# Transposing the MLP's pre-activation instead of computing it a second time, in the first phase of a two-layer decoder kernel

## The reference

```
z    = x @ w1.T + b1                # 512 hidden features
pred = silu(z) @ w2.T + b2
e    = pred - v
grad_w2, grad_b2  from e and silu(z)
dz   = (e @ w2) * silu'(z),  grad_w1, grad_b1  from dz and x
w   <- (1 - alpha) * w - theta * grad
```

## Time and profile before

| what | value |
|---|---|
| median of three runs | 1011.18 us (1008.25 to 1017.53) |
| the profiled execution's own time | 1009.8 us |
| its span | 1008.1 us |
| mean granted TensorE clock, share of full speed | 0.863 |
| busy: PE / DVE / ACT / POOL | 745.5 / 527.1 / 383.9 / 163.0 us |
| TensorE's weight loads (PEld), beside PE | 481.1 us |
| first phase | 0 to 270 us |
| gradient loop of step 0 / 1 / 2 / 3, from its first product | 59.68 / 125.96 / 186.21 / 248.73 us |

### The profile page before, as it was taken

The page is one execution under the profiler, slowest core; times in us unless marked ns, Lnnn a source line. Parts: engine busy times, 40 slices in busy tenths (PEclk is TensorE's granted clock), DMA queues, the critical chain, the costliest instruction groups (busy, mean ns, idle before and its releaser), DMA issues.

```text
span 1008.1 us, 13899 instructions
## 1 busy us (share of the span) xinstructions
PE 745.5 (74%) x4570; PEld 481.1 (48%) x4570; DVE 527.1 (52%) x1934; ACT 383.9 (38%) x888; POOL 163.0 (16%) x207
## 2 busy tenths in 40 slices
PE   5788796887865986985984972999357568667665
PEld 4445354453422662662662751778336336344342
DVE  4435245252625945945946821111245784876865
ACT  3514436144222542542540541333024354344543
POOL 9300000000111005005004004000331411311020
PEclk8889899898966997997995985999787889788887
DMA  7500000010024026026024001141110100200000
GB/s 213 181 1 21 2 21 0 10 42 0 11 48 105 1 49 100 11 47 98 12 44 55 2 1 61 27 108 44 48 40 2 46 7 13 52 11 12 0 12 10
DMA packets 49246, 39.49 MB, mean 39 GB/s; under 512 B 11235, under 2 KB 42659, under 8 KB 49189
## 3 DMA queue, kind: packets, MB, share of 16 engines
q1 hardware_dynamic: 47140, 34.62, 15.7%
q0 software_dynamic: 2048, 4.20, 1.5%
HBM read 27.20 MB, written 11.60 MB: 38 GB/s over the span
## 4 chain that ended last, share of the span: by engine, by line
PE 54%; DVE 23%; issue 8%; ACT 7%; DMA 5%; SPq 2%; POOL 1%; DVEq 0%; ACTq 0%; POOLq 0%
PE bank L1247 4%; PE bank L1236 4%; PE bank L1349 3%; DVE R L2182 3%; DMA q_stack<-parts_dram 3%; PE bank L1130 2%; PE bank L990 2%; PE bank L1133 2%; PE bank L1143 2%; PE bank L1132 2%; PE bank L922 2%; DVE bank L1900 2%; PE bank L1102 2%; PE bank L1013 2%; PE bank L1050 2%
## 5 line engine op out<-in xcount | busy, mean ns | idle before, releaser
L1900 DVE CUSTOM_DVE_ANT_0 bank<-bank,add_q 128x256 f32<-128x256 f32 x256 | 100.1, 456 | 34.7 <-PE bank L1102 21.6
L1558 ACT ACTIVATE pT<-bank 128x512 f32<-128x512 f32 x128 | 76.1, 597 | 75.7 <-PE bank L1133 73.4
L1102 PE MATMUL bank<-k_stack,q_stack 96*128 96x256 bf16 x256 | 51.7, 300 | 31.0 <-DMA q_stack<-parts_dram 24.2
L1349 PE MATMUL bank<-XT,kpad 128*128 128x256 f32 (+1 forms) x256 | 60.8, 368 | 15.9 <-DVE cT L2124 15.9
L1130 PE MATMUL bank<-q_stack,k_stack 96*128 96x256 bf16 x256 | 70.3, 275 | 1.8 <-DVE mx L1900 1.8
L1132 PE MATMUL bank<-add_k,ident_b 128*128 128x256 bf16 x256 | 70.6, 276 | 0.0
L1133 PE MATMUL bank<-neg_max,head_sel 96*128 96x256 bf16 x256 | 70.5, 275 | 0.0
L1349 PEld LDWEIGHTS bank<-XT,kpad 128*128 128x128 f32 x256 | 49.9, 217 | 26.1 <-DVE cT L2124 17.7
L2124 DVE TENSOR_TENSOR cT<-bank,decay 128x384 f32<-128x384 f32 x64 | 35.1, 554 | 48.5 <-POOL decay L872 28.3
L1583 ACT ACTIVATE he<-bank 128x324 f32<-128x324 f32 x64 | 28.2, 441 | 69.4 <-PE bank L1236 63.9
L872 POOL TENSOR_SCALAR_AFFINE_SELECT decay<-decay 128x256 f32<-128x256 f32 x64 | 27.2, 426 | 159.5 <-ACT decay L1652 159.5
(11 more groups left out here) (412 smaller groups left out, 1680.8 us busy)
## 6 DMA issues: line engine op xcount, KB each, us to landing
k_stack<-parts_dram SPq DMA_DIRECT2D x48, 64.0 KB
q_stack<-parts_dram SPq DMA_DIRECT2D x24, 128.0 KB, 8.1
expert_in<-no_rows SPq DMA_DIRECT2D x8, 324.0 KB, 4.0
rows<-expert_in SPq DMA_DIRECT2D x8, 324.0 KB
expert_out<-rows_y SPq DMA_DIRECT2D x8, 324.0 KB
moe_w<-in_L_ffn_w_dram SPq DMA_DIRECT2D x1, 2048.0 KB
parts_dram<-k_parts SPq DMA_DIRECT2D x4, 384.0 KB, 2.8
parts_dram<-q_parts SPq DMA_DIRECT2D x12, 128.0 KB, 1.7
```

What stands on the lines that cost most here:

```text
L1102: last = pe.matmul(q_bank(n)[:, c * S:(c + 1) * S], q_stack[:, h // 2, b * S + c * P:b * S + (c + 1) * P], k_stack[:, h // 2, h % 2, b * S ...
L1349: last = pe.matmul(c_bank(n)[:, lo:lo + width], kpad2[:, h, b * S + c * P:b * S + (c + 1) * P], XT[:, par, q0:q0 + width], start=True, sto ...
L1558: act.activation(pT[:, g % 2, j], k_bank(n)[:].rearrange("p (c q) -> p c q", c=QC), ACT.Exp).then_inc(exp_ready.sem, 1)
L1900: last = dve.tensor_tensor_reduce(sc, sc, add_q[:, b * QC + c, :], 1.0, 2.0 * NEG, ALU.add, ALU.max, mx[:, c, h:h + 1])
```

## The change

z in feature layout, bias included, now stays in a tile of its own, zs, 512 + 64 tokens wide; hT gets silu of it. `z_and_dh` fills its PSUM bank by four transposes of 128 x 128 blocks of zs instead of the f32 product and the bias product. The bias parts go: their tiles, their DMA, their zeroing, VectorE's five instructions and TensorE's wait for them. VectorE's wait for masks_made stands after the first phase now. In step 0 ScalarE writes the memory tokens' z by four Identity activations, waits for its own last one, and then takes four Silu; z_copied counts one more there, and TensorE waits for it in step 0 ahead of the loop.

```diff
--- before.py
+++ after.py
@@ -208,19 +208,18 @@
         swa_ready = signal("swa_ready", 1, extra=1)
         vT_copied = signal("vT_copied", 1, extra=1)
         zT_a = signal("zT_a", FC, extra=1)
-        z_copied = signal("z_copied", FC)
+        z_copied = signal("z_copied", FC, extra=1)
         hT_a = signal("hT_a", FC, extra=FC)
         pred_a = signal("pred_a", 1)
         e_ready = signal("e_ready", 1)
         eT_tr = signal("eT_tr", 1)
         etok_copied = signal("etok_copied", 1, extra=1)
         zd_ready = signal("zd_ready", NC, extra=1)
-        b1_split = signal("b1_split")
         sg_ready = signal("sg_ready", NC, extra=1)
         dz_ready = signal("dz_ready", NC, extra=1)
         grads_ready = signal("grads_ready", NC, extra=1)
         grads_added = signal("grads_added", 1)
-        dve_a = signal("dve_a", 2 * NU + 2 * NC, extra=2 + 1 + 2 + 3)
+        dve_a = signal("dve_a", 2 * NU + 2 * NC, extra=2 + 1 + 2)
         upd_pe = signal("upd_pe")
         upd_dve = signal("upd_dve")
         updated = signal("updated")
@@ -407,10 +406,7 @@
         grad1 = sb("grad1", [P, HID], scope=scope_a)
         grad2 = sb("grad2", [P, HID], scope=scope_a)
         grad_b = sb("grad_b", [P, FC + 1], scope=scope_a)
-        b1_row = sb("b1_row", [1, HID], scope=scope_a)
-        b1_rest = sb("b1_rest", [1, HID], scope=scope_a)
-        b1_mid = sb("b1_mid", [1, HID], BF16, scope=scope_a)
-        b1_parts = sb("b1_parts", [96, HID], BF16, scope=scope_a)
+        zs = sb("zs", [P, FC, T + M], scope=scope_a)
 
         stage = ExitStack()
         qT = sb("qT", [P, T], scope=stage)
@@ -587,7 +583,6 @@
             (w2T[:], a["L0_attn_w2T"].rearrange("(k p) d -> p k d", p=P)),
             (b1[:], a["L0_attn_b1_cols"]),
             (b2[:], a["L0_attn_b2"].unsqueeze(1)),
-            (b1_row[:], a["L0_attn_b1"].unsqueeze(0)),
             (rate[:, 0:1], a["L0_attn_alpha"].partition_broadcast(P)),
             (rate[:, 1:2], a["L0_attn_theta"].partition_broadcast(P)),
             (xtok[0:M, NC, :], a["L0_attn_mem"]),
@@ -787,7 +782,7 @@
             pool.iota(iota_e[:], pattern=[[1, E]], base=0, channel_multiplier=0, allow_small_or_imprecise_dtypes=True)
             pool.iota(first_slot[:], pattern=[[SLOTS, E]], base=0, channel_multiplier=0, allow_small_or_imprecise_dtypes=True)
             pool.iota(trash[:], pattern=[[P, PAIRS]], base=E * SLOTS, channel_multiplier=1, allow_small_or_imprecise_dtypes=True)
-            for t in (b1_parts, q_stack, k_stack, neg_max, neg_pm, v_aug, seen, fb_parts):
+            for t in (q_stack, k_stack, neg_max, neg_pm, v_aug, seen, fb_parts):
                 pool.memset(t[:], 0.0)
             pool.memset(ones16[:], 1.0)
             made = Chain(pool, masks_made, 0)
@@ -946,7 +941,7 @@
                     pe.wait_ge(*pTb_copied.at(i, u + 1))
                     wait_apart(pe, passed, *pTa_copied.at(i, u + 1))
                     if c is None:
-                        pe.wait_ge(*z_copied.at(i))
+                        pe.wait_ge(*z_copied.at(i, FC))
                     heads = [(h, slice(DH0 * h, DH0 * h + DH0)) for h in range(H0)]
                     if c is None:
                         for h, r in heads:
@@ -1009,12 +1004,13 @@
                         pe.wait_ge(*dz_ready.at(i, c - 2))
                     if c >= 2:
                         pe.wait_ge(*sg_ready.at(i, c - 1))
-                    x_c = xin[:, c // QC, M + (c % QC) * P:M + (c % QC + 1) * P] if c < NC else xin[:, 0, 0:M]
-                    pe.matmul(zb[0:n], x_c, w1T[:], start=True, stop=False)
-                    pe.matmul(zb[0:n], row_sel[:, 0:n], b1_parts[:], start=False, stop=True)
+                    cols = slice(c * P, c * P + n)
+                    for k in range(FC):
+                        pe.transpose(zb[0:n, k * P:(k + 1) * P], zs[:, k, cols], ident[:])
                     pe.matmul(db[0:n], eT[:, c * P:c * P + n], w2[:], start=True, stop=True).then_inc(zd_ready.sem, 1)
 
-                pe.wait_ge(*b1_split.at(0))
+                if is_first(i):
+                    pe.wait_ge(*z_copied.at(i))
                 for c in range(3):
                     z_and_dh(c)
                 pe.wait_ge(*xtok_loaded.at(i))
@@ -1469,18 +1465,22 @@
                         exponentials(u + 2)
                     if u < FC:
                         act.wait_ge(*zT_a.at(i, u + 1))
-                        act.activation(hT[:, u, 0:T], bank[1][:], ACT.Identity, bias=b1[:, u:u + 1]).then_inc(z_copied.sem, 1)
+                        act.activation(zs[:, u, 0:T], bank[1][:], ACT.Identity, bias=b1[:, u:u + 1]).then_inc(z_copied.sem, 1)
                 act.wait_ge(*pv_a.at(i))
                 act.copy(oT[:, 0:T], bank[7][:]).then_inc(oT_copied.sem, 1)
                 if is_first(i):
                     act.copy(oT[:, T:T + M], bank[1][:, 0:M]).then_inc(oT_copied.sem, 1)
-                act.wait_ge(*z_copied.at(i))
+                act.wait_ge(*z_copied.at(i, FC))
                 for k in range(FC):
-                    act.activation(hT[:, k, 0:T], hT[:, k, 0:T], ACT.Silu).then_inc(hT_a.sem, 1)
+                    act.activation(hT[:, k, 0:T], zs[:, k, 0:T], ACT.Silu).then_inc(hT_a.sem, 1)
                 if is_first(i):
                     act.wait_ge(*zT_a.at(i))
-                for k in range(FC if is_first(i) else 0):
-                    act.activation(hT[:, k, T:T + M], bank[1][:, M * (k + 1):M * (k + 2)], ACT.Silu, bias=b1[:, k:k + 1]).then_inc(hT_a.sem, 1)
+                    for k in range(FC):
+                        last = act.activation(zs[:, k, T:T + M], bank[1][:, M * (k + 1):M * (k + 2)], ACT.Identity, bias=b1[:, k:k + 1])
+                    last.then_inc(z_copied.sem, 1)
+                    act.wait_ge(*z_copied.at(i))
+                    for k in range(FC):
+                        act.activation(hT[:, k, T:T + M], zs[:, k, T:T + M], ACT.Silu).then_inc(hT_a.sem, 1)
                 if is_first(i):
                     act.wait_ge(*swa_ready.at(i))
                     act.copy(vT_mem[:], bank[2][:, 0:M]).then_inc(vT_copied.sem, 1)
@@ -1764,14 +1764,6 @@
                     chain.link(dve.scalar_tensor_tensor(eT[:, T:T + M], bank[4][:, 0:M], b2[:, 0:1], vT_mem[:], ALU.add, ALU.subtract))
                     last = dve.tensor_scalar(eT[:, T:T + M], eT[:, T:T + M], float(B), None, ALU.mult)
                 last.then_inc(e_ready.sem, 1)
-                if is_first(i):
-                    dve.wait_ge(load_w.sem, 16 * len(loads_w))
-                    dve.wait_ge(*masks_made.at(0))
-                    chain.link(dve.tensor_copy(b1_parts[0:1, :], b1_row[:]))
-                    chain.link(dve.tensor_tensor(b1_rest[:], b1_row[:], b1_parts[0:1, :], ALU.subtract))
-                    chain.link(dve.tensor_copy(b1_mid[:], b1_rest[:]))
-                    dve.tensor_copy(b1_parts[32:33, :], b1_mid[:])
-                    dve.tensor_tensor(b1_parts[64:65, :], b1_rest[:], b1_mid[:], ALU.subtract).then_inc(b1_split.sem, 1)
                 for c in range(chunks(i)):
                     n, s = (P if c < NC else M), c % 2
                     dve.wait_ge(*sg_ready.at(i, c + 1))
@@ -1811,6 +1803,7 @@
             last.then_inc(updated.sem, 1)
 
             dve.wait_ge(late_loaded.sem, 16 * len(late_w))
+            dve.wait_ge(*masks_made.at(0))
             pro = Chain(dve, dve_pro, 0)
             pro.link(dve.tensor_copy(fb_parts[0:1, :], ffn_b[:]))
             pro.link(dve.tensor_tensor(fb_row[:, 0], ffn_b[:], fb_parts[0:1, :], ALU.subtract))
```

## The result

In 20 runs each, shared over chips, the changed kernel takes 1005.95 us (1002.32 to 1014.92) and the kernel before 1011.94 (1003.27 to 1017.68). The ratio is 0.9946, interval 0.9924 to 0.9967, so the gain is 5.5 us, 3.3 to 7.7. The forecast was 1001, with a gain of 9.1 as its sum. Its direction held and the range of 994 to 1007 holds the time, but the size was too large by more than the measurement is uncertain.

The account below looks back on a forecast made before the run. Each stretch has its own bound; the gradient loop is TensorE's, with the ScalarE and VectorE chain close behind. Gains of 3.3 (step 0), 3.4 (steps 1 and 3) and 2.4 (step 2) sum to 9.1: 1001 us, range 994 to 1007.

Parts of the forecast that it names:

- The prices: TensorE's gradient loop: four transposes 0.42 us in the stream instead of z with bias at 1.08, saving 0.66 per chunk.
- The far bound of 0.66: Four transposes priced like f32 products reloading weights, 0.165 us each; the gain would be 6.9, the time 1003.
- Block 0 hangs on dz of chunk 0: First gradient block, steps 1 and 3: TensorE waits 0.9 us for dz; block 0 starts 1.03 earlier.
- the chunk between blocks counts in full: Chunk 3 in steps 1 and 3: 0.66 us gained, the dz chain staying behind with 0.5 slack.
- Step 0's two edits: Ahead of step 0's loop: no bias-parts wait gains 0.95 us, doubled memory-token activations cost 0.9; net nothing.
- if the clock does the same at the same time: Loops of steps 2 and 0: low clock assumed at the same moments as before, giving gains of 2.4 and 3.3 us.
- The dz chain is the bound: Rival: ScalarE and VectorE take 0.5 us more, hiding the gain of five chunks between blocks; time 1004, chance 0.10.
- The low clock hits all four loops: Rival: steps 1 and 3 meet low clock like step 2, 2.0 us lost; time 1003, chance 0.12.
- More counts: Rival: the low clock misses the loops of steps 0 and 2, 1.8 us more gained; time 999, chance 0.14.
- The fall to 1.2 GHz inside the loop: Rival: transposes replacing streaming columns halve the clock in the chunk loop; time about 1061, chance 0.04.
- the page's rule: Trainium skill page: transposes don't engage the full clock; by it the fourth rival's sum, or mildly the third's.
- At nothing: Bias row's DMA (0.34 us) and GpSimd's setup with zeroing, beside step 0's attention, among items priced at no gain.

Follow-up runs that it names:

- Experiment 1: Kernel before and changed kernel, each ended behind the first phase's weights' update, later phases left out: 278.70 and 273.39 us.
- experiments 5 and 6: Changed kernel ended behind the first phase, with a needless product in the idle ahead of block 0 (272.09 us), or five needless ScalarE activations in step 0 (273.77 us).
- the cut kernel: The changed kernel ended behind the first phase's weights' update, all later phases left out: 273.39 us.
- the filled ones: Kernels ended behind the first phase, two needless products per step in TensorE's wait for the Silus: 267.07 us on the changed kernel, 273.13 on the kernel before.

## Why the prediction was right and wrong

- **The prices were right.** Four transposes 0.43 in the stream and 0.46 from idle; forecast 0.42 and 0.49. The far bound of 0.66 was not needed.
- **The shape of the loop was right.** Block 0 hangs on dz of chunk 0, the chunk between blocks counts in full, no idle before the third block. A step at full clock gains 1.52, not the 1.69 forecast; block 0, now started from idle, takes 134.18 - 131.27 = 2.91 instead of 2.83, and its start is 0.07 later.
- **Step 0's two edits** nearly cancelled, as said: w2 1.03 later, of which the added activations are 0.73 (4.95 instead of 4.22 behind the output product) and a longer attention 0.3; the loop 0.29 earlier, 0.6 counted from the output product, where nothing was forecast.
- **The step that failed** is "if the clock does the same at the same time", in steps 2 and 0: the forecast took low clock that one execution had met in these loops as part of their price. It booked 2.4 for step 2 and 3.3 for step 0. By its own terms at full clock they would have been 1.7 and 2.35, and the sum 7.4. At full clock they measured 1.5 (17.1 to 15.6) and 2.2 (22.16 to 19.99), so that the change's own gain in the loops is 6.7. Of the 9.1, then, 1.7 were the low clock's and 0.7 the small sizes above. The measured interval of 3.3 to 7.7 holds 6.7 and not 9.1. The silent other half of the step was that the attention costs what it cost. In the profiled pair the loops did escape the low clock and gained 10.1, but the three attention stretches took 89.9 against 85.9. Experiment 1 puts the shortfall into the first phase, with the same median low time on both sides. That the place of the low clock follows the timing is argued from experiments 5 and 6, and not shown.
- **One sum of the forecast does not come out.** With 0.55 us at full clock from 186.21 on, four transposes of 0.49 end at 186.70 and not at 186.85; that is 0.15 of the 2.4. The row read for it does not say on which side the full clock lay, either: by narrower windows the low clock held from 186.4 to 189.8.
- **The rivals.** "The dz chain is the bound" fell: no new idle stands before the third block. "The low clock hits all four loops" fell: in the whole kernel's profiled execution none was hit, in the cut kernel's one of four. "More counts" had the loops right and the sum wrong, since it too left the attention alone. The fall to 1.2 GHz inside the loop did not come, and with these two the page's rule fails here in both of its forms.
- **At nothing** held for the bias row's DMA and GpSimd: the attention of step 0 takes 37.5 against 37.1, and no wait on either appears.

What stays open: whether a loop with less TensorE work raises the chance of a low stretch behind it at all, or only its place. The kernels with transposes in the loop have attention sums of 86.7 to 90.3, the others in the old order 84.2 to 90.5, one profiled execution each; that is too little to tell. Without the filled ones they are 88.2 to 90.3 against 84.2 to 87.1, but there the others met more low clock in their loops. Which stretch meets the low clock, and why, stays open. The 1.6 that the phases behind the first gave back in the profiled pair is one pair too, within the scatter.

## What to carry to other kernels

A stretch that runs at the low clock in one trace is not a fixed cost of that stretch: price an edit at full clock on both sides, and put the low clock into the range, for the whole neighbourhood that the edit shifts. Where TensorE waits in each step, work that needs nothing from the wait (here the transposes) belongs into it; here it was paid twice, once off the path (3.3 us a step) and once by the clock (1.7). When a product's second layout comes cheap out of its first, see also that its inputs are early, and move it, instead of leaving it where the product stood.

## What the runs showed that was not expected

- Two f32 products of 1.7 us that compute nothing, in a wait of 2.4 us, took 10.5 us off the whole kernel (1011.99 to 1001.49). In the profiled pair 4.6 of the 7.3 lie in the first phase.
- A delay of 1.6 us on the path of step 0 cost 0.4 us in the median, within the scatter, and its profiled execution had the low clock in other stretches.
- Two cut kernels that differ only in one product inside an idle showed the same low-clock pattern to the tenth (0.89, 1.00, 0.89). Yet the executions of either differ among each other in mean clock (0.906 to 0.920 and 0.912 to 0.927), so the pattern is not fixed by the program's timing alone.
- A product by the identity in f32 takes two instructions a block and 0.89 us for four blocks; transpose mode takes one each and 0.43.
